# Graph network kernel: the three bf16 parts of the basis coefficients summed in PSUM instead of on VectorE

## The reference

```
W_rel = einsum('rb,bio->rio', w_comp, weight)     # 64 types, 16 bases
h_all = einsum('ni,rio->nro', x, W_rel)
msg   = h_all[src, etypes] * norm                 # norm: one weight per edge
agg   = segment_sum(msg, dst, num_segments=N)
```

## Time and profile before

| what | value |
|---|---|
| median of 3 runs | 1011.59 us (1010.98 to 1013.21) |
| profiled execution | 1010.13 us, its span 1008.6 us |
| mean granted TensorE clock | 0.935 of full speed |
| PE matmuls busy | 805.6 us (80%) |
| DVE busy | 737.5 us (73%) |
| POOL busy | 443.6 us (44%) |
| ACT busy | 357.0 us (35%) |

### The profile page before, as it was taken

How to read it: one execution, slowest core, us unless ns; L and a number is a source line. 1 busy time by engine, 2 the same in 40 slices (tenths; PEclk the granted TensorE clock), 3 DMA queues, 4 the chain that set the end, 5 groups by cost and what they waited for, 6 DMA issues and landing times.

```text
span 1008.6 us, 27165 instructions
## 1 busy us (share of the span) xinstructions
PE 805.6 (80%) x5567; PEld 581.8 (58%) x5571; DVE 737.5 (73%) x2438; ACT 357.0 (35%) x708; POOL 443.6 (44%) x532
## 2 busy tenths in 40 slices
PE   3667776767896999999449889988888889887876
PEld 2522232222454999999337667666666667555545
DVE  7979999999764554435437777777677778888884
ACT  0502457788883000002324454444343332222100
POOL 2013323223000000011177777777777777777772
PEclk9789989899875999999759999999999999999998
DMA  4012345566442000012682212221211122212122
GB/s 120 1 38 81 104 116 129 139 152 156 116 107 51 2 1 2 1 33 77 199 251 52 55 52 52 52 52 52 53 53 52 52 52 52 54 53 52 52 52 83
DMA packets 64847, 73.24 MB, mean 73 GB/s; under 512 B 12803, under 2 KB 53178, under 8 KB 64666
## 3 DMA queue, kind: packets, MB, share of 16 engines
q1 hardware_dynamic: 48362, 37.30, 13.7%
q0 software_dynamic: 16432, 35.29, 13.3%
HBM read 43.85 MB, written 8.22 MB: 52 GB/s over the span
## 4 chain that ended last, share of the span: by engine, by line
PE 37%; DVE 23%; issue 14%; DVEq 9%; POOL 8%; DMA 6%; SPq 2%; ACT 1%; POOLq 0%; ACTq 0%
PE ps L1074 14%; PE ps L1141 12%; POOL CT L564 8%; PE ps L999 5%; DMA CT<-h_dram,src_col 5%; DVE ohbuf L761 5%; DVE CT L880 4%; DVE CT L883 2%; DVE u L761 2%; DVEq L883 2%; PE ps L1121 2%; DVEq L123 2%; DVE coef_sum L732 2%; DVEq L880 1%; DVE ohbuf L756 1%
## 5 line engine op out<-in xcount | busy, mean ns | idle before, releaser
L564 POOL DMA_INDIRECT CT<-h_dram,src_col x391 | 369.8, 946 | 125.2 <-issue 97.2
L1141 PE MATMUL ps<-CT 128*128 128x256 f32 x1180 | 306.0, 408 | 64.2 <-DVE CT L880 32.9
L1141 PEld LDWEIGHTS ps<-CT 128*128 128x128 f32 x1180 | 205.9, 193 | 158.9 <-issue 140.3
L883 DVE SCALAR_TENSOR_TENSOR CT<-ps,dlP,CT 128x256 f32<-128x256 f32 x580 | 279.4, 482 | 4.5
L880 DVE COPY CT<-CT 128x128 f32 x590 | 146.9, 249 | 121.7 <-PE ps L1141 62.6
L1282 ACT COPY CT<-ps 128x256 f32<-128x256 f32 x200 | 77.8, 389 | 310.3 <-PE ps L1141 306.3
L999 PE MATMUL ps<-ohbuf 128*128 128x400 bf16 x395 | 119.1, 384 | 35.7 <-DVE ohbuf L761 14.1
L1221 ACT CAST stage<-ps 128x800 bf16<-128x800 f32 x100 | 82.4, 824 | 95.0 <-PE ps L999 94.6
L1074 PE MATMUL ps<-u,CT 128*128 128x192 bf16 x1250 | 108.0, 249 | 6.3 <-DVEq L811 6.3
L519 POOL DMA_DIRECT2D u<-types_dram x49 | 32.7, 672 | 181.1 <-PE ps L1007 167.1
L1074 PEld LDWEIGHTS ps<-u,CT 128*128 128x128 bf16 x1250 | 104.6, 99 | 8.6 <-DVEq L811 7.8
(11 more groups left out here) (173 smaller groups left out, 652.7 us busy)
## 6 DMA issues: line engine op xcount, KB each, us to landing
CT<-stage SPq DMA_DIRECT2D x200, 100.0 KB, 3.2
u<-types_dram POOLq DMA_DIRECT2D x49, 128.0 KB, 3.5
CT<-h_dram,src_col POOLq DMA_INDIRECT x391, 2.5
coef_dram<-coef_out POOLq DMA_DIRECT2D x49, 64.0 KB, 3.6
CT<-coef_dram SPq DMA_DIRECT2D x1, 3048.0 KB, 10.8
out<-CT SPq DMA_DIRECT2D x4, 256.0 KB
ohbuf<-x SPq DMA_DIRECT2D x3, 320.0 KB, 3.7
x_dram<-ohbuf SPq DMA_DIRECT2D x3, 320.0 KB, 2.4
```

What stands on the lines that cost most here:

```text
L564: pool.indirect_dma_start(out=gring[:, (j + 1) % GRING, :], out_offset=None, in_=h2_dram, in_offset=bass.IndirectOffsetOnAxis(ap=src_col[: ...
L883: dve.scalar_tensor_tensor(kpair[:, u, :, :], nodes.unsqueeze(1).broadcast_to([P, BASES, WIN]), dl, coef_flat[:, ds(tiles * -BASES + NT * ...
L1141: pe.matmul(ps[:, ds(summed.place(counts[u][0], RING), 1), 0:WIN * BASES], gpair[:, u, :], kpair[:, u, :, :].rearrange("p b d -> p (b d)") ...
```

## The change

PE adds the three parts itself. `wc_parts` is laid out part by part, and for each of the four pieces of a chunk PE issues three matmuls of 32 columns, one for each part, which accumulate in the same 32 columns of PSUM. `sum_parts` and its buffer go; `finish_coefs` multiplies by the edge weight straight out of PSUM. PE now waits with chunk `c` for `coef_cp`, that `finish_coefs` is done with chunk `c - 1`.

```diff
-        wc_parts = sb("wc_parts", [P, 2, BASES, PARTS], BF16)
+        wc_parts = sb("wc_parts", [P, PARTS, 2, BASES], BF16)
...
-                step(dve.tensor_copy(wc_parts[:, :, :, 0], wc_sb[:]))
-                step(dve.tensor_tensor(wc_rest[:], wc_sb[:], wc_parts[:, :, :, 0], ALU.subtract))
+                step(dve.tensor_copy(wc_parts[:, 0], wc_sb[:]))
+                step(dve.tensor_tensor(wc_rest[:], wc_sb[:], wc_parts[:, 0], ALU.subtract))
...
-            def sum_parts(c):
                 dve.wait_ge(coef_mm, c + 1)
-                if not (isinstance(c, int) and c == 0):
-                    dve.wait_ge(coef_cp, c)
-                dve.tensor_reduce(coef_sum[:], ps[:, COEF_BANK, 0:CCH * BASES * PARTS].rearrange("p (n k) -> p n k", k=PARTS),
-                                  AX.X, ALU.add).then_inc(coef_read, 1)
-
-            def finish_coefs(c, b, stored):
-                dve.wait_ge(coef_read, c + 1)
...
-                                  coef_sum[:].rearrange("p (i h b) -> p i h b", h=2, b=BASES),
+                                  ps[:, COEF_BANK, 0:CCH * BASES].rearrange("p (i h b) -> p i h b", h=2, b=BASES),
...
-                    if u == COEF_SUM and coefs:
-                        sum_parts(c - 1)
...
-                            pe.wait_ge(coef_read, c)
+                            pe.wait_ge(coef_cp, c)
                         pe.wait_ge(typed, c + 1)
                         for i in range(CCH // 2):
-                            n = 2 * BASES * PARTS
-                            last = pe.matmul(ps[:, COEF_BANK, i * n:(i + 1) * n], cbuf[:, phase, i * P:(i + 1) * P],
-                                             wc_parts[:].rearrange("p h b k -> p (h b k)"), start=True, stop=True)
+                            n = 2 * BASES
+                            for k in range(PARTS):
+                                last = pe.matmul(ps[:, COEF_BANK, i * n:(i + 1) * n], cbuf[:, phase, i * P:(i + 1) * P],
+                                                 wc_parts[:, k].rearrange("p h b -> p (h b)"), start=(k == 0),
+                                                 stop=(k == PARTS - 1))
                         last.then_inc(coef_mm, 1)
```

More of the change, by code:

```diff
@@ L77 @@
 COEF_MM = 6
-COEF_TYPES, COEF_SUM, COEF_OUT = 4, 7, 9
+COEF_TYPES, COEF_OUT = 4, 9
 CHALF = CCH * P // 2
@@ L191, in build @@
         wc_sb = sb("wc_sb", [P, 2, BASES], F32)
-        wc_parts = sb("wc_parts", [P, 2, BASES, PARTS], BF16)
+        wc_parts = sb("wc_parts", [P, PARTS, 2, BASES], BF16)
         wc_rest = sb("wc_rest", [P, 2, BASES], F32)
-        coef_sum = sb("coef_sum", [P, CCH * BASES], F32)
         coef_out = sb("coef_out", [P, HALVES, CCH * BASES], F32)
@@ L344, in build @@
         coef_mm = sem("coef_mm")
-        coef_read = sem("coef_read")
         coef_cp = sem("coef_cp")
@@ L709, in finish_h @@
                 dve.wait_ge(ld_par, 64)
-                step(dve.tensor_copy(wc_parts[:, :, :, 0], wc_sb[:]))
-                step(dve.tensor_tensor(wc_rest[:], wc_sb[:], wc_parts[:, :, :, 0], ALU.subtract))
-                step(dve.tensor_copy(wc_parts[:, :, :, 1], wc_rest[:]))
-                step(dve.tensor_tensor(wc_parts[:, :, :, 2], wc_rest[:], wc_parts[:, :, :, 1], ALU.subtract))
+                step(dve.tensor_copy(wc_parts[:, 0], wc_sb[:]))
+                step(dve.tensor_tensor(wc_rest[:], wc_sb[:], wc_parts[:, 0], ALU.subtract))
+                step(dve.tensor_copy(wc_parts[:, 1], wc_rest[:]))
+                step(dve.tensor_tensor(wc_parts[:, 2], wc_rest[:], wc_parts[:, 1], ALU.subtract))
                 dve.wait_ge(hmul, H_TURNS)
@@ L726, in type_rows, with finish_coefs @@
                 dve.tensor_scalar(cbuf[:, b, :], cbuf[:, b, :], typ[:, 0:1], None, ALU.is_equal).then_inc(typed, 1)
-            def sum_parts(c):
+            def finish_coefs(c, b, stored):
                 dve.wait_ge(coef_mm, c + 1)
-                if not (isinstance(c, int) and c == 0):
-                    dve.wait_ge(coef_cp, c)
-                dve.tensor_reduce(coef_sum[:], ps[:, COEF_BANK, 0:CCH * BASES * PARTS].rearrange("p (n k) -> p n k", k=PARTS),
-                                  AX.X, ALU.add).then_inc(coef_read, 1)
-            def finish_coefs(c, b, stored):
-                dve.wait_ge(coef_read, c + 1)
                 if stored is not None:
```

## The result

The kernel after takes 1014.43 us (median of 17 runs, 1012.78 to 1016.3), the kernel before 1012.53 us in the same comparison (17 runs, 1010.78 to 1013.96). The ratio is 1.0022 with a 95% interval of 1.0015 to 1.003: the change costs about 2.2 us. The forecast was 1012.2 us, range 1009.3 to 1017.0. The result lies 2.2 us above it, of which 0.9 us are the kernel before, which measured 1012.53 us here and 1011.59 us when the forecast was made; the change was put at 0.6 us and cost about 1.3 us more.

A forecast was written before the change was run, and what follows sets the result against it. The prediction took PE's instruction stream, 4.16 us a turn, to bound the coefficient turns. All terms were 0 except 0.6 us for issuing eight more pairs: 1011.59 + 0.6 = 1012.2 us, range 1009.3 to 1017.0.

The forecast's parts named there:

- the likeliest case: PE's stream sets the pace as before, price of the added pairs 0 to 1.3 us: 1010.2 to 1014.2 us, chance 0.70.
- the slower rival: Between pairs 6 and 7, more small matmuls cost PE their issue: up to 8 us more, likeliest 2 to 5; chance 0.18.
- PE's instruction stream is the bound: In the coefficient turns PE's register and issue work, 4.16 us a turn, sets the pace, not its array or DVE.
- DVE's 22.5 us are worth nothing on the path: Dropping DVE's reduction, 0.46 us in each of 49 turns, gains 0, since PE does not wait for DVE.
- Multiplication out of PSUM at 0: DVE's multiplication by the edge weight costs nothing more from PSUM (291 ns) than from SBUF (292 ns).
- wait for `coef_cp` at 0: At the coefficients PE waits only if DVE leads by less than about 1.6 us; it leads by 2.16: 0.
- accumulation: Rival: each accumulating coefficient matmul waits for the one before, 49 x 1.2, near 60 us more, 1070; chance 0.03.
- The array's time is hidden: Twelve coefficient matmuls take the array 0.17 to 0.33 us more a turn, covered by the next group's register work: 0.
- The issue of eight more pairs: Eight more pairs of load and matmul a turn in PE's stream, 49 turns: taken at 0.6 us, half of 1.3.
- the row in the same place: First coefficient load to pair 7's, 0.22 against 0.21 us: eight pairs cost at most 0.027 us a turn, 1.3 in all.
- the other one: Bound from 50 pairs in a row: at most 19 ns a pair, 7.4 us for eight pairs in 49 turns.
- two signs: Three PE turns take over 12.6 us at full clock; the first turn without coefficients comes later by the whole difference.

The follow-up runs named there:

- the wide kernel: Kernel after with twelve matmuls of 96 columns in place of 32, all three parts as moving operand each time: 1014.84 us, ratio 1.0015.
- the six kernels: Kernels before, after and four follow-ups, by span of 48 turns: 201.5, 201.1, 202.0 us with four coefficient matmuls a turn, 204.0, 203.9, 204.2 with twelve.
- PE's part alone: Kernel before with twelve matmuls of 32 columns for four of 96, each into its own columns, DVE still adding the parts: 1013.71 us, ratio 1.0015.

## Why the prediction was right, and the size that was off

The result lies in the range, but not where the forecast had its weight: 1014.43 us is above the 1010.2 to 1014.2 of the likeliest case, and the ratio of 1.0022 is slower by just over 0.2%, which had a chance of 0.22 against 0.70 for within 0.2%. That the range held owes to the slower rival that it was stretched for.

*PE's instruction stream is the bound.* Right. With DVE relieved alone nothing clear of the noise was won (0.9993), and the turns stayed as they were. The change loses 2.2 us where PE's turn is the longer one (before and after) and wins 8.2 us where, without the fourth group, it has become the shorter.

*DVE's 22.5 us are worth nothing on the path.* Right: they became waiting at L747, 23.7 us of it where there were 3.0 (at L756).

*Multiplication out of PSUM at 0, wait for `coef_cp` at 0, accumulation.* Right: the kernel with the first two and without the twelve matmuls is level with before; the one with the twelve and without the accumulation loses as much as the whole change.

*The array's time is hidden.* Right, for the reason given: 0.20 us more of it, in the wide kernel, left nothing behind. The Trainium skill (TensorE: Matmul & The Clock Gate, "Wait — 56ns, not 53.3ns?") gives some 25 ns as the least from one matmul's start to the next; the twelve starts in 0.31 us agree with it. Shown in full it would have cost 6.4 us, an estimate of the prediction by that page, and the runs show that it did not.

*The issue of eight more pairs* is the term that was mis-sized. It was taken at 0.6 us, half of the bound of 0.027 us a turn that the row in the same place gave. It measured 0.052 us a turn, 2.5 us in 48 turns (2.3 by the means of the six kernels): about twice that bound, a third of the 7.4 us of the other one. The rows of PE's weight loads at the same place say where the first bound went wrong, after and then before (the row that followed):

```profile
64.71 0.31 PEld L988 LDWEIGHTS ps<-u 128*128 128x128 bf16 x2 [0.41 <-issue]
65.05 0.42 PEld L997 LDWEIGHTS ps<-wc_parts,u 128*128 128x128 bf16 x12
65.39 0.10 PEld L988 LDWEIGHTS ps<-u 128*128 128x128 bf16 x1
65.85 0.31 PEld L988 LDWEIGHTS ps<-u 128*128 128x128 bf16 x2 [0.36 <-issue]
```

```profile
65.92 0.10 PEld L999 LDWEIGHTS ps<-u 128*128 128x128 bf16 x1 [0.44 <-issue]
```

From the first coefficient load to pair 7's it is now 0.34 us for 0.22; from the third group to pair 8 it is 1.14 us (64.71 to 65.85) for 1.09 (64.83 to 65.92). So 0.12 us late at pair 7, and 0.05 us still late at pair 8, which the prediction said would be on time. As medians over the passes of the loop, third group to pair 8 takes 1.14 us for 1.09 in the loop's second turn and 1.14 for 1.07 in its third; in the first it takes 1.09 us in both kernels, and pair 8 is on time. The row of before showed a place where four pairs fitted beside the register work for pair 7; it could not price the pairs that no longer fit. The records of PE's register instructions around this place say the same: from the wait with the coefficients to the next register instruction it is 117 ns with four pairs and 186 ns with twelve (both are the medians over all turns, too):

```
before  102.712 ALU_OP L1004   102.829 ALU_OP L980
after   102.836 ALU_OP L993    103.022 ALU_OP L969
```

That is 69 ns for eight pairs, 8.6 ns each, in the second and third turn of the loop, and the turn grows by some 65 ns; in the first it is 147 ns, 30 more, and the rest of the turn gives them back. The prediction's rival "more small matmuls cost PE their issue" named this mechanism, with 5 ns a pair as the point from which it decides and 2 to 5 us as its likely price. Of its two signs, one came clearly: the first turn without coefficients comes later by the whole difference (its register load stands 201.2 us behind that of the first turn in the loop before, 203.6 after). The other, three turns over 12.6 us, could not decide, since the kernel before has a stretch of 12.64. The case that was forecast and this rival are one mechanism at two prices, and the measured price lies on the rival's side, at its lower end.

## What to carry to other kernels

An engine that is busy for 99.5% of a stage need not be its bound: look at whether the engine behind it waits, and whether the lead between them grows; here it grew where PE was the bound, and stayed at 1.9 us once DVE was. Work moved to the engine whose instruction stream sets the pace costs its issue, however idle that engine's array is, and the relief on the other side turns into waiting. Make the stream of the slower engine shorter first; here one group less a turn turned the same change from a loss of 2.2 us into a gain of 8.2.

A row that shows a few instructions fitting beside other work bounds the cost of those few, not of more of them.

## What the runs showed of the hardware

A register load on PE takes 0.333 us for four words, but 0.81 to 0.87 us (medians) for three, wherever the row starts. For nine it takes 2.2 to 3.1 us, but 0.85 to 1.1 us where the first word has a number in the table that is a multiple of four. A word costs 0.27 to 0.29 us in a load of three and 0.24 to 0.35 in the slow loads of nine, against 0.08 in a load of four; why is open. A fourth word that nobody uses made the kernel 29 us faster (1030.35 to 1001.41 us).

Twelve matmuls of 32 columns, each with its own weight load and three at a time into the same columns, start within 0.31 us, though each lasts 177 ns: accumulation in the same columns does not make them wait for one another. Where nothing accumulates, twelve take 0.30 us (103.42 to 103.72 in the kernel with PE's part alone).
